# GraphSAGE-style max aggregation over 25 neighbours: the opening and the uses of a group rearranged, and the last late round taken into the loop

## What is computed

```
h = relu(layernorm(x))                      # per node, 128 features
mask = adj != 0
idx = the first S = 25 columns with mask set, for each row
agg = max over the valid idx of h[idx]      # -inf where a row has none
agg = where(degree <= 25, max(agg, 0), agg)
out = relu(concat(h, agg) @ W + b)
result = x + out
```

## Time and profile before

| | |
|---|---|
| median of 3 runs | 721.28 us |
| the profiled execution | 721.64 us |
| its span in the trace | 719.9 us |
| mean granted TensorE clock | 0.974 of full speed |
| PE busy, DVE busy | 84%, 82% |
| ACT busy, POOL busy | 59%, 12% |

### The profile page before, as it was taken

One profiled execution on the slowest core, in us unless ns is written; L12 is line 12 of the kernel. 1 busy time (PEld: TensorE's weight loads), 2 busy tenths in 40 slices (PEclk: granted clock), 3 DMA queues, 4 the chain that ended last, 5 costly groups with the idle time before them and its releaser, 6 DMA issues.

```text
span 719.9 us, 9712 instructions
## 1 busy us (share of the span) xinstructions
PE 603.5 (84%) x2736; PEld 243.4 (34%) x2736; DVE 589.2 (82%) x705; ACT 425.4 (59%) x579; POOL 85.6 (12%) x134
## 2 busy tenths in 40 slices
PE   0555689998999898989899898989798989998976
PEld 0110234343343333434343333343343434342323
DVE  5221398989989799898989799898989898989986
ACT  0555583868268482687568583777478763856210
POOL 3000000401021100311022100311031100311010
PEclk9996799999999999999999999999999999999999
DMA  9883753656744474555945575566744462231100
GB/s 262 299 233 126 232 198 74 216 169 238 183 146 172 111 270 123 183 178 166 270 135 188 124 254 140 204 185 204 224 175 160 126 210 47 78 142 42 46 15 15
DMA packets 107905, 118.04 MB, mean 164 GB/s; under 512 B 74452, under 2 KB 94167, under 8 KB 103383
## 3 DMA queue, kind: packets, MB, share of 16 engines
q1 hardware_dynamic: 107862, 117.61, 52.2%
HBM read 58.85 MB, written 20.97 MB: 111 GB/s over the span
## 4 chain that ended last, share of the span: by engine, by line
PE 43%; DVE 18%; ACT 13%; issue 10%; DMA 8%; SPq 7%; DVEq 1%; ACTq 0%
PE picked L607 14%; PE picked L608 12%; DVE best L787 6%; PE ring L554 6%; DMA x_in<-in_x_dram 5%; PE side L565 3%; DVE hot L774 3%; PE side L566 3%; DVE best L793 3%; ACT late_rank L445 3%; DVE late_hot L799 3%; SPq L269 3%; ACT late L460 2%; ACT mask L440 2%; ACT chosen L455 2%
## 5 line engine op out<-in xcount | busy, mean ns | idle before, releaser
L787 DVE TENSOR_TENSOR best<-picked,best 128x1024 f32<-128x1024 f32 x224 | 271.0, 1219 | 71.5 <-PE picked L608 70.5
L607 PE MATMUL picked<-hot,h_hi 128*128 128x512 f16 x512 | 198.6, 388 | 21.7 <-DVE best L787 11.3
L608 PE MATMUL picked<-hot,h_lo 128*128 128x512 f16 x512 | 197.5, 386 | 0.0
L607 PE MATMUL picked<-late_hot,hi_skew 128*128 128x512 f16 x344 | 131.5, 382 | 24.6 <-DVE late_hot L799 12.8
L608 PE MATMUL picked<-late_hot,lo_skew 128*128 128x512 f16 x344 | 131.3, 382 | 0.0
L793 DVE TENSOR_TENSOR best<-picked,best 128x1024 f32<-128x1024 f32 x86 | 105.1, 1223 | 16.6 <-PE picked L608 15.5
L445 ACT ACTIVATE late_rank<-ring,late_bias 128x512 bf16<-128x512 f32 x128 | 81.7, 686 | 56.4 <-PE ring L554 53.2
L445 ACT ACTIVATE rank<-ring,late_bias 128x512 bf16<-128x512 f32 x128 | 87.4, 687 | 40.4 <-PE ring L554 39.9
L455 ACT ACTIVATE chosen<-side,bias_cut 128x512 bf16<-128x512 f32 x128 | 87.3, 682 | 35.6 <-PE side L566 35.6
L774 DVE TENSOR_SCALAR hot<-rank 128x4096 f16<-128x4096 bf16 x64 | 88.0, 1377 | 23.2 <-ACT rank L445 23.2
L484 ACT COPY best<-picked 128x1024 f32<-128x1024 f32 x32 | 32.5, 1014 | 118.8 <-PE picked L608 118.8
(11 more groups left out here) (73 smaller groups left out, 407.3 us busy)
## 6 DMA issues: line engine op xcount, KB each, us to landing
adj_in<-in_adj_dram SPq DMA_DIRECT2D x15, 2048.0 KB, 7.9
kept<-chosen SPq DMA_DIRECT2D x128, 128.0 KB, 3.3
picks<-kept SPq DMA_DIRECT2D x15, 1024.0 KB, 5.0
late_skew<-late SPq DMA_DIRECT2D x32, 192.0 KB, 2.4
x_in<-in_x_dram SPq DMA_DIRECT2D x8, 512.0 KB, 9.0
xres<-in_x_dram SPq DMA_DIRECT2D x16, 256.0 KB, 2.6
late_skew<-late SPq DMA_DIRECT2D x16, 256.0 KB, 2.6
late_skew<-late SPq DMA_DIRECT2D x32, 128.0 KB, 2.3
```

Of the source, the lines that this page charges most:

```text
L607: nc.tensor.matmul(dst, hi[:, slot, k, :], onehot, start=start, stop=False)
L608: return nc.tensor.matmul(dst, lo[:, slot, k, :], onehot, start=False, stop=stop)
L787: nc.vector.tensor_tensor(best[:, half, s, :, :], picked[s][:, :, :], best[:, half, s, :, :], ALU.max).then_inc(picked_read, 1)
```

## The change

It moves work between uses and rewrites the opening; only SP's loop and the projection's arithmetic stay as they are.

- Late rounds: the count is max(L, 1), all of them run in the loop, and each makes the one-hots of a further round, the last one too. PE's wait for the one-hots is raised by one per group for it.
- Selection of group g+2 at uses 8 to 15, ranking of g+1 at 6 to 13, late one-hots after 11 and 13, late members found two pairs behind use 14 and two behind use 15. Late ranks 4 to 7 follow pairs 4 and 5; the counting goes into `final` behind pairs 6 and 7, its maximum behind use 8.
- Statistics after uses 9 and 10, moments after 12, gain at the end of the even group, normalizing on POOL ahead of the folding of the count, ReLU at use 7.
- Opening: constants ahead of the masks, masks of groups 1 and 2 on DVE, group 1 selected between the steps of group 0, its transposed mask held in `rank[:, 1]`.

```diff
-    SELECT_WITH, RANK_WITH = spread_over(5, 12), spread_over(4, 11)
-    LATE_EARLY, LATE_REST_USE, COUNT_USE, LATE_HOT_USES = 6, 4, 4, (9, 11)
-    LATE_USES, RELU_USE = (12, 13, 14, 15), 12
-    STATS_USES, MOMENTS_USE, GAIN_USE = (13, 14), 15, 5
+    SELECT_WITH, RANK_WITH = spread_over(8, 15), spread_over(6, 13)
+    LATE_EARLY, LATE_WITH, COUNT_WITH, COUNT_USE, LATE_HOT_USES = 4, {4: (4, 5), 5: (6, 7)}, (6, 7), 8, (11, 13)
+    LATE_USES, RELU_USE = {14: (0, 1), 15: (2, 3)}, 7
+    STATS_USES, MOMENTS_USE = (9, 10), 12
...
+            def first_turns(g, turned):
+
+                for q in range(Q):
+                    sp.wait_ge(mask_made, Q * g + q + 1)
+                    sp.dma_start_transpose(turned[:, :, q * P:(q + 1) * P], mask[:, q, :]).then_inc(mask_turned, 16)
...
+            first_turns(0, mask_t)
             load_adj(1, 1)
             load_adj(2, 0)
-            sp.reg_add(chosen_due, chosen_due, K)
-            for k in range(K):
-                sp.wait_ge(chosen_made, k + 1)
-                sp.dma_start(kept_by_block[k], chosen[:, k, :]).then_inc(first_stored[k // HALF], 16)
+            for k in range(2):
+                first_store(k)
+            first_turns(1, rank[:, 1])
+            for k in range(2, K):
+                first_store(k)
                 if k == K - 2:
                     first_picks(0)
             first_picks(1)
-            turn_masks()
             load_adj(3, 1)
+            first_turns(2, mask_t)
             skew_h(0, 0)
             skew_late(0)
             sp.wait_ge(first_loaded, 32)
             store_chosen(True)
             load_picks(K)
-            turn_masks()
...
-                    nc.gpsimd.tensor_scalar(late_other[:, c:c + 1], late_most[c * PART:c * PART + 1, :], LINK * P / 2 - 1, 1.0, ALU.add,
+                    nc.gpsimd.tensor_scalar(late_other[:, c:c + 1], late_most[c * PART:c * PART + 1, :], LINK * P / 2, 1.0, ALU.add,
                                             ALU.max).then_inc(late_folded, 1)
...
-                fold_count(u % 2)
-                if not at_end(it, u, 1):
+                more = not at_end(it, u, 1)
+                if more and u % PER_BATCH == PER_BATCH - 1:
+                    normalize(batch_of(it, u + 1))
+                fold_count(u % 2 if more else 0, u % 2)
+                if more:
                     if u % PER_BATCH == PER_BATCH - 1:
-                        normalize(batch_of(it, u + 1))
                         low_part(batch_of(it, u + 1), ((u + 1) // PER_BATCH) % 2)
...
             for k in range(K):
                 choose(0, k)
-            make_masks(1, range(Q))
             turned_h(0, 0)
-            act.wait_ge(consts_made, 3)
+            for k in range(HALF):
+                choose(1, k)
             for k in range(K):
                 stage(0, k, rank[:, 0], late_bias[:, 0:1])
             find_late(0, 0, K)
             for s in range(2):
                 first_maxima(0, s, 0)
-            for p in range(1, PAIRS):
-                find_late(p, 0, K)
-            for k in range(K):
-                choose(1, k)
+                choose(1, HALF + s)
+            find_late(1, 0, K)
+            choose(1, HALF + 2)
+            find_late(2, 0, K)
+            choose(1, HALF + 3)
+            find_late(3, 0, K)
...
                 pe.reg_add(rounds_done, rounds_done, n)
-                done = pe.snap(rounds_done)
-                late_round(g, done, 0, slot)
-                pe.reg_add(rounds_done, rounds_done, 1)
...
                 project(g, it, u, new_batch)
-                if more:
-                    for k in range(4, LATE_EARLY):
-                        late_ranks(g + 1, at + LATE_AT, k)
-                    if not at_end(it, u, 2):
-                        pe.wait_ge(chosen_made, K * (g + 3))
-                    count(g + 1)
...
                 dve.reg_add(rounds_done, rounds_done, n)
-                done = dve.snap(rounds_done)
-                for i in range(2):
-                    take_late(s, i, done, 0)
-                dve.reg_add(rounds_done, rounds_done, 1)
...
                 finish_group(g, s, 16 * (it * (UNROLL // 2) + u // 2 + 1))
+                if ahead:
+                    make_gain(batch_of(it, u) + 1)
```

132 lines of the change are left out of this document (69 added, 63 removed).

## The result

The kernel after the change takes 758.6 us in the median of four runs (758.3 to 761.9), against 721.5 us (721.0 to 723.3) before on the same chip: a ratio of 1.052, interval 1.0485 to 1.0554. It is slower, as forecast, but by 37 us where I had forecast 25, and the time lies just above the range's end of 758. The profiled execution took 758.3 us, 756.6 of them span.

The account below looks back on a forecast made before the run. DVE was taken as the bound, PE close beside it, with x's load lacking slack. Waits for x 36.6, opening -9.5, last three groups -1.8 sum to +25.3 on 721.64, 746.9, median 746.5 us; range 733 to 758 (own range 738 to 753).

Parts of the forecast that it names:

- Rival (a): Even groups and group 12: x doesn't bind, so the statistics don't wait; 40 us less, 706 us; chance 0.07.
- Rival (b): x's load lands in 3.9 us everywhere, 5.1 less in five groups; 721 us, no change; chance 0.04.
- (c): The opening gains nothing, as the skew of late members comes no earlier than before; 756 us; chance 0.12.
- 7.2 us of a pair: Loss per odd and even group together: 0.9 for x's later issue, 5.95 behind its landing, 0.35 for the clock.
- SP: x issued at T+28.7: SP's queue: x issued 28.7 us after the end of use 13's maximum (27.8 before), behind transposes, skews and output store.
- After landing: 11.45 and 0.35 for the clock: Even groups: DVE has 11.45 us from x's landing to the first late maximum; half clock on PE adds 0.35.
- Rival (d): PE's clock stays low after each wait, four uses at 3.0 us instead of 1.9; 765 us; chance 0.04.
- ACT, finds before selection 7: T+7.0: Odd group's end: selection 7 queues behind two finds; first late maximum 7.0 us after use 13's maximum ends, +1.8.
- POOL: +1.75 on T: POOL's second product blocks use 5's one-hot, 1.75 us lost; use 13's maximum ends 26.0 after the last late maximum starts.
- Late rounds: Only group 11 loses a round (3.88 us); first unused one-hot fits a 0.66 us wait, the second delays folding 0.47.
- Rival (e): The last round's unused one-hots cost their full 1.4 us, ten groups counting; 755 us; chance 0.05.
- Opening: -9.5: Group 0's first late maximum comes about 95.5 instead of 105.03, 9.5 us sooner; bounds 0 to -15.

Follow-up runs that it names:

- stats_back: The kernel after the change with the statistics put back behind uses 13 and 14 and the moments behind 15: 721.1 us, ratio 0.999.
- x_early: The kernel after the change, statistics still early, but x loaded before the odd group's stores, once the earlier x is used up: 707.8 us, ratio 0.980.
- after_select_5: The kernel after the change with the selection back at uses 5 to 12, ranking left at 6 to 13: 738.7 us, ratio 1.024.
- stats_early_alone: The kernel before the change with only the statistics moved to uses 9 and 10 and the moments to 12: 745.6 us, ratio 1.032.
- after_finds_last: The kernel after the change, x still late, with all four finds of late members behind use 15: 756.8 us, ratio 1.047.
- hot_at_7: x_early_finds with the one-hots of rank 4 made after use 7 instead of use 5: 699.3 us, ratio 0.968.
- before_loop_round: The kernel before the change with only the last late round taken into the loop, so max(L, 1) rounds and unused one-hots: 721.8 us, ratio 0.999.
- round_outside_2: x_early_finds with the last late round outside the loop again, without unused one-hots, each half waiting for its own buffer: 692.0 us, ratio 0.957.
- x_early_finds: x_early with all four finds of late members behind use 15: 695.0 us, ratio 0.964.
- opening_order: x_early_finds with group 0's finds ahead of the last chosen blocks on ACT, and its late skew ahead of the h skews: 692.4 us, ratio 0.958.

## Why the prediction was wrong in size

**The deciding mechanism was right.** x's landing took the place of DVE's maxima, in the groups forecast. Group 5's x left 345.59 and the statistics began 8.74 us later. stats_back and x_early show it from both sides. The mean wait for x in groups 2 to 10 was 7.9 us (forecast 7.1) and DVE's own arrival was at A+18.0 (forecast 17.9). One of the three waits that the prediction read from the earlier trace rows was the opening's own load; only groups 2 and 10 waited by more than 0.1 us. Rival (a) is what x_early makes true: 707.8 us against 706 worked out. That this is so close is luck in part: by the folds of the profiled executions the five pairs gave 6.6 us where (a) had 0.9, the pair 11+12 lost 0.3 where (a) gained 2.9, and the first fold came 8.5 us sooner instead of 9.5. Rival (b) is out, since x landed 8.7 to 10.3 us after its issue in groups 2 to 10, and so is (c).

**The step that failed: the 7.2 us of a pair (0.9 for SP, 5.95 behind the landing, 0.35 for the clock).** With the 6.5 of groups 4 and 8 that is 6.9 in the mean, and it was 8.5. Measured from A in the means over five pairs, x's issue moved by 1.6 us (forecast 0.9), the time from there to the first statistics by -0.5 (forecast -0.3), the stretch from the statistics to the first late maximum by 7.4 (forecast 6.3), and the late rounds by 0.1.

**SP: x issued at T+28.7. Mis-sized.** It was T+30.2 in group 5 (T is 25.42 after A at 289.94), and T+30.6 in the mean. The step took the length of SP's fixed chain from the earlier trace rows, with transposes of 5.38 us, and missed that the selection brings picks and the skew of late to one moment. The transposes took 6.53 us, and started at T+11.3 instead of T+10.75. In the medians picks, 1 MB, 5.0 us to landing before, took 6.5; the skews of 192 KB 4.9 instead of 2.4. In after_select_5, with earlier masks and shorter transposes, x leaves 2.5 us earlier. The reading of T was off too: the earlier trace rows give (4.82 - 1.22) / 3 = 1.20 us from maximum to maximum and not 1.135, and use 13's maximum ended at 309.34 and not 309.14.

**After landing: 11.45 and 0.35 for the clock. Mis-sized.** The first number is good (11.33 in x_early), but the stretch came out 12.35 to 13.44, 1.0 to 2.1 longer instead of 0.35. PE's first row behind group 6's wait, and windows of the kernel after from there:

```profile
356.39 0.61 PE L626 MATMUL picked<-hot,h_hi 128*128 128x512 f16 x1 [6.16 <-DVE best L800]
```

```profile
356.30:360.30 4.00, 3.91 (x10) 1.44 (x11) 4.00 (x14) 1.37 (x2) 0.00 (x0) 0.50 0.00 0
360.30:362.30 2.00, 2.00 (x9) 0.75 (x8) 1.29 (x6) 0.67 (x2) 0.00 (x0) 0.73 0.18 66
```

PE ran at half clock for its first 5.0 us (356.4 to 361.4), where the prediction had taken 4 from the earlier trace rows, and ten matmuls in 4.00 us filled them. I had counted only its pairs; with the selection at uses 8 to 15 each use also carries two or three matmuls for selection and ranking, and those doubled too.

Both are needed for the lengthening, as the kernel after shows itself:

| group | 0 | 12 | 4 | 2 | 8 | 6 | 10 |
|---|---|---|---|---|---|---|---|
| half clock once PE works again, us | 0 | 0 | 3.2 | 3.7 | 4.4 | 5.0 | 5.8 |
| statistics to first late maximum, us | 11.42 | 11.36 | 12.35 | 12.53 | 12.94 | 13.21 | 13.44 |

At full clock the late selection's matmuls cost nothing (x_early has 11.33 as well, and group 0 had a wait of 1.8 us), and the longer the clock stays low, the longer the stretch. With fewer matmuls left for it the same half clock costs less: stats_early_alone has 4.7 us of it in group 6 and needs 11.17, 0.3 more than its 10.84 at full clock; after_select_5, where only the selection is as early as in the kernel before, needs 12.0 in the mean. So the selection accounts for about half of the lengthening; that ranking two uses later is the rest was not tried. Rival (d), the clock staying low, was wrong: it was back at full 3.2 to 5.8 us after PE's restart in each of groups 2 to 10. The Trainium skill (TensorE: Matmul & The Clock Gate, "HAM oscillation") describes a cold start behind every wait for a transfer, and the trace agrees: half clock behind each of the five waits of 6.3 to 9.8 us. It does not say that the clock then stays low for four uses, so it spoke for the forecast's own clock term as much as for (d), and the price lay between the two, 1.0 to 2.1 us.

**ACT, finds before selection 7: T+7.0. Right in kind.** In group 5 chosen block 7 stood behind two finds on ACT and ended at T+4.2 (forecast 3.8). PE waited for it:

```profile
319.60 0.66 PE L621 MATMUL side<-eye,h 128*128 128x128 f32 x4 [2.04 <-ACT chosen L473]
```

Measured from T the first late maximum comes at 7.4 to 7.5 us in groups 7, 9 and 11 and at 8.7 to 9.0 in 1, 3, 5 and 13, where the 2.04 us of PE's wait were followed by half clock (0.64 granted from 319.60 to 324.30). The prediction charged nothing for it in front of x, since it took x's issue from T and not from A, and 1.8 us in group 13. The first was right: in after_finds_last group 5 ends 2.7 us sooner after the fold in front, and x leaves only 0.5 us sooner. The second was too little: the same run gets 2.6 us back in group 13, so that the last three groups gained 0.3 us and not 1.8.

**POOL: +1.75 on T. Right as a row, wrong as a price.** The 2.69 us are in the trace, 1.47 more than the 1.22 of the others. The terms of T add up to +0.3, which the prediction called no change, and without the two collisions they would have given 2.4 us and not the 0.8 it names. T came at A+25.42 (forecast 26.0), 0.8 sooner than before (309.34 - 283.11 = 26.23) although the collision is there. hot_at_7 removes the blocking in all seven places and no odd group ends sooner: the selection's chain ends later anyhow. The rule of the Trainium skill (SBUF — State Buffer, "Who interferes with whom"), by which the one that starts first keeps the shared port, agrees with the rows (POOL's product ran from 301.19 to 303.09, the one-hot from 301.48); it just had no bearing on the time.

**Late rounds: right.** 84 late maxima and 116 late one-hots are in the trace; before_loop_round and round_outside_2 show the one-hots free. Rival (e) is out. The fold does come 0.46 us later with them, but PE's chain to the next pairs runs from the last late maximum.

**Opening: -9.5. Measured -8.3** (first late maximum at 96.76 against 105.03), because the skew left at 62.7 instead of 61.6. By the first fold, behind the second unused one-hot, it is -7.7. PE's wait for that skew:

```profile
68.69 1.04 PE L572 MATMUL ring<-late_skew,half_w 128*128 128x512 bf16 x2 [8.01 <-DMA late_skew<-late]
```

**Sum.** Five pairs at 8.5 instead of 6.9 us make 8.1 us of the miss, the last three groups 1.5, the opening at its first fold 1.8; these are the 11.4 us by which the spans moved more than forecast (the medians: 12). Of the 1.6 us of a pair about 1.1 are the stretch behind the landing and 0.7 x's later issue, less 0.2 for the time from issue to statistics. The range failed because its bounds moved each term by itself. The selection's delay, the crowded queue and the half clock all press on the same stretch, and I had let SP's issue vary by 1 us only. That the selection's place enlarges both is shown by after_select_5, which takes 3.0 of the 8.5 us back; the rest of the miss behind the landing was not taken apart by a run.

## What to carry to other kernels

When an operation is moved forward, look first at when its input lands, and count what will stand behind the wait: the loss is the work that used to run while the transfer was under way. A gain made ahead of a transfer that does not depend on it is given back at its landing, so move the transfer first and tune the rest after; here the same edit was worth 13 us then and 2 before. Where a step's cost is read from one group, look at the other kind of group too: the crowded queue stood in the kernel before already, one group further on. A blocked or wasted instruction has a price only if its engine's chain ends last in that stretch.

## What I had not expected of the hardware

- Transfers on one queue slow each other by their spacing: with the skews 0.5 us behind the 1 MB of picks (all groups from 1 on in the kernel after), four transposes took 6.4 to 6.9 us to issue and 192 KB took 4.9 us to land in the median; with 2.4 us between them it was 5.4 and 2.6 us. The spacing doesn't explain all: in three of thirteen groups of after_finds_last the transposes took 6.1 to 6.5 us with 1.9 or 2.4 us between. What slows them was not looked into.
- The same idle of PE, 3.1 us in the same place, left the clock at full in x_early_finds and at 0.54 in opening_order, and so returned a gain of 1.7 us made 430 us earlier. Elsewhere 2.3 us of idle were enough in one kernel and 2.4 us were not in another. Differences of 1 to 2 us between two versions can be this, and nothing in the code.
